# Twenty-four attention stages in two attention layers: a loop on the engines over the heads, or straight code

## The chip, the cores and the metric

The kernel runs on one core of a Trainium2 chip. A core has five engines that work side by side, each from an instruction stream of its own: TensorE (PE, matrix products; its weight loads are listed as PEld), VectorE (DVE), ScalarE (ACT), GpSimd (POOL) and SyncE (SP, which here issues the DMA transfers). They meet only through semaphores. The metric is the time of one execution on the device in microseconds (us): the median over runs, lower is better.

## The reference, cut to what matters

The input is x, of shape (2, 48, 48, 384). Two attention layers follow each other, each on a group-normalised x and with a residual:

```
x = x + attention0(group_norm(x))   # 7x7 neighbourhood mask, 16 registers as further keys
x = x + attention1(group_norm(x))   # all 2304 tokens, biases from relative positions
```

Each layer projects to queries, keys and values for 12 heads of 32 numbers, takes a softmax over the scores, weights the values with it and projects back. The first is called the local attention below, the second the full attention. With 12 heads and a batch of 2, each has 24 pairs of head and batch element: the 24 stages that this text is about.

## The kernel before, in words

The kernel is a row of phases: normalisation and projection, local attention, output mixing, then the same again with position biases and the full attention. Each phase is a block in which every engine has a stream of its own.

A stage is numbered `n = h * B + b` (head h, batch element b, B = 2). What the two attentions have in common is this. The queries of a stage are worked through in 6 units of 384. PE computes scores in two matmuls for each key tile (lines 896 and 897 local, 1570 and 1572 full). ACT takes the exponential out of PSUM (line 1047 local, 24 times a stage; line 1672 full, 54 times a stage). DVE and POOL form the low half of the probabilities (lines 1089 and 1704). PE multiplies high and low half with the values (lines 935/936 and 1596/1597). Between these, PE and DVE already find the row maxima of the next stage (lines 874/1107 and 1543/1715), so that the stages overlap, and the last steps of a stage are done within the next one.

In the local attention a row of maxima goes back to the operand `q_b` of the scores by DMA. SP issues it at line 821, in three transfers, right behind the loads of the next stage's queries, keys and values (lines 768 to 777) and the store of the last result (line 804). PE waits for it on the first scores of a stage (line 896, semaphore `rows_in`). In the full attention this row is copied by ACT (line 1660) and needs no DMA.

The order of each engine's work is the order of the code. What walks over the stages is `each_stage` (line 55), which every engine calls: SP, PE, ACT, DVE and POOL, in each of the two attentions. It writes out the stages of head 0 and of head 11 (n = 0, 1, 22, 23). The stages of heads 1 to 10 (n = 2 to 21) are a loop that runs on the engine: its body is two stages long, is written once, and is run ten times. At its end stands a conditional branch back to its start, taken nine times in each attention. Within the body the head is a register. A semaphore value or an address that depends on it has to be computed by register instructions first; these and the branch are listed under the line 59 and the lines of the waits.

Of the kernel before, what the change touches and what calls it, by code (L numbers as in the profile page):

```python
# [14 lines left out]
B, SIDE, C = 2, 48, 384  # L15
TOK = SIDE * SIDE
ALL = B * TOK
HEADS, D = 12, 32
# [35 lines left out]

def each_stage(engine, stage):

    for b in range(B):
        stage(0, b)
    with engine.Fori(1, HEADS - 1) as h:
        for b in range(B):  # L60
            stage(h, b)
    for b in range(B):
        stage(HEADS - 1, b)


def window_of(tile, size, limit):
# [583 lines left out]
def attention(nc, ctx, x, values, layer, dram, sem):  # L650
# [104 lines left out]
    with nc.Block() as block:  # L755
        @block.sync
        def _(sp):
# [80 lines left out]
            def stage(h, b):  # L838
# [12 lines left out]
                if not is_last(n):  # L851
                    place_rows(n + 1, 1 - b, False)

            each_stage(sp, stage)
            store(HEADS - 1, 1)
            for b in range(B):
# [4 lines left out]
        def _(pe):  # L861
# [149 lines left out]

            pe.wait_ge(consts_in, CONSTS)
            each_stage(pe, stage)
            for k in range(STEPS - LAG, STEPS):
                use(STAGES - 1, 1, k)
# [3 lines left out]
        def _(act):  # L1019
# [29 lines left out]
            def stage(h, b):  # L1049
                n = h * B + b  # L1050
                for k in range(STEPS):
# [3 lines left out]
                    if (k - LAG) % PER_UNIT == PER_UNIT - 1:  # L1055
                        if u >= 0:
                            take_result(h, b, u)
                        elif not is_first(n):
                            take_result(h - (1 - b), 1 - b, NA + u)

            each_stage(act, stage)
            for a in range(NA - (LAG - 1) // PER_UNIT - 1, NA):
                take_result(HEADS - 1, 1, a)
# [957 lines left out]
```

## Time and profile before

| | before |
|---|---|
| median of 3 runs | 3359.76 us (3355.78 to 3362.64) |
| the profiled execution | 3359.43 us, its span 3357.2 us |
| PE busy | 2895.1 us, 86% of the span |
| DVE busy | 2494.8 us, 74% |
| POOL / ACT busy | 57% / 55% |
| local attention, stages 2 to 21 | 331.5 to 719.85 us |
| full attention, stages 2 to 21 | 1433.0 to 3089.6 us |
| TensorE clock granted, mean over the span | 0.941 of full speed |

The page lists for each engine how long it was busy. Register, branch and semaphore instructions are not counted as busy, so an engine that is held up by its own instruction stream looks idle. In the lists of waits such time has the name "issue": the engine waited for nothing that the profile shows. A stage's start is taken here as the start of its first exponential on ACT. A window of the trace gives, for a stretch, the busy time of PE, PEld, DVE, ACT and POOL with the number of instructions, then the granted TensorE clock, the share of the DMA engines' time in use, and GB/s.

Two DMA queues called "instruction", q8 and q14, carry instructions and no data: q8 in packets of 16 KB, q14 in packets of mostly 8 KB.

### The profile page before, as it was taken

Reading aid. Unit: us, or ns where it says so; the run is one execution under the profiler, and the core shown is the slowest. Engines: PE = TensorE matmul, PEld = TensorE weight load, DVE = VectorE, ACT = ScalarE, POOL = GpSimd, SP = SyncE. Lnnn points to the kernel's source line nnn. Section 1 sums busy time; section 2 is a strip of 40 time slices with the busy share of each in tenths; the row PEclk is TensorE's granted clock in tenths of the full one; section 3 lists DMA queues with packets and bytes.
Section 4 is the critical chain, followed back from the end, with each engine's and each line's share of the span. In section 5 each row is a group of like instructions: output and inputs, shape, how many; then the busy total and the mean of one; then the engine's idle time right before and its main releaser. Section 6 shows DMA issues by size and latency. Waiting matters only on the chain. (4 is left out here: it accounts for less than half of the span.)

```text
span 3357.2 us, 94851 instructions
## 1 busy us (share of the span) xinstructions
PE 2895.1 (86%) x34200; PEld 1947.2 (58%) x34200; DVE 2494.8 (74%) x5171; ACT 1862.9 (55%) x3434; POOL 1903.2 (57%) x1561
## 2 busy tenths in 40 slices
PE   1996999997199748999999999999999999999977
PEld 1554677773155625666666666666666666666644
DVE  6745888876654537888787888888888888888854
ACT  3333666774333425666565666656565666566654
POOL 3452555550303006777777777777777777777762
PEclk9996999998599559999999999999999999999989
DMA  2425565547121984222222222222222222222114
GB/s 115 178 87 132 139 145 132 139 117 258 45 119 58 245 185 136 49 50 50 50 50 50 50 50 50 50 50 53 47 58 48 56 49 56 46 57 59 22 41 142
DMA packets 162461, 294.95 MB, mean 88 GB/s; under 512 B 78522, under 2 KB 112404, under 8 KB 156564
## 3 DMA queue, kind: packets, MB, share of 16 engines
q1 hardware_dynamic: 162052, 289.43, 33.9%
q8 instruction: 265, 4.34, 0.6%
q14 instruction: 144, 1.18, 0.1%
HBM read 189.37 MB, written 85.45 MB: 82 GB/s over the span
## 5 line engine op out<-in xcount | busy, mean ns | idle before, releaser
L1704 POOL TENSOR_TENSOR fprob_low<-fprob 128x768 f16<-128x768 f32 x1008 | 1449.7, 1466 | 563.3 <-ACT fprob L1672 562.8
L1715 DVE TENSOR_REDUCE fpart_max<-fmax_acc 128x1 f32<-128x384 f32 x2592 | 1363.8, 556 | 368.7 <-PE fmax_acc L1543 353.0
L1672 ACT ACTIVATE fprob<-fscores 128x768 f32<-128x768 f32 x1296 | 1048.2, 809 | 768.7 <-PE fscores L1572 768.6
L1543 PE MATMUL fmax_acc<-fk_m,fq_m 128*128 128x384 f16 x2592 | 853.2, 330 | 146.0 <-ACT fq_b L1660 104.8
L1570 PE MATMUL fscores<-fq_a,fk_a 128*128 128x384 f16 x2592 | 848.2, 327 | 39.5 <-issue 31.5
L1572 PE MATMUL fscores<-fq_b,fk_b 97*128 97x384 f16 x2592 | 851.4, 328 | 4.2 <-issue 4.2
L1596 PE MATMUL fout_acc<-fv,fprob 128*128 128x65 f16 x7776 | 612.0, 191 | 2.6 <-POOL fprob_low L1704 2.1
L1597 PE MATMUL fout_acc<-fv,fprob_low 128*128 128x33 f16 x7776 | 596.0, 179 | 0.9 <-issue 0.9
L1596 PEld LDWEIGHTS fout_acc<-fv,fprob 128*128 128x128 bf16 x7776 | 543.2, 97 | 68.4 <-POOL fprob_low L1704 5.1
L1597 PEld LDWEIGHTS fout_acc<-fv,fprob_low 128*128 128x128 f16 x7776 | 487.9, 96 | 52.5 <-issue 2.6
L1543 PEld LDWEIGHTS fmax_acc<-fk_m,fq_m 128*128 128x128 f16 x2592 | 251.9, 97 | 336.7 <-DVE fpart_max L1715 121.1
L1089 POOL TENSOR_TENSOR prob_low<-prob 128x242 f16<-128x242 f32 (+2 forms) x360 | 250.0, 717 | 257.1 <-ACT prob L1047 256.3
L1572 PEld LDWEIGHTS fscores<-fq_b,fk_b 97*128 97x128 f16 x2592 | 252.6, 97 | 160.9 <-issue 5.1
L1570 PEld LDWEIGHTS fscores<-fq_a,fk_a 128*128 128x128 f16 x2592 | 252.2, 97 | 135.1 <-issue 42.8
L1704 DVE TENSOR_TENSOR fprob_low<-fprob 128x768 f16<-128x768 f32 x288 | 274.7, 954 | 7.5 <-ACT fprob L1672 7.5
L1107 DVE TENSOR_REDUCE tile_max<-max_acc 128x1 f32<-128x282 f32 (+3 forms) x432 | 176.5, 435 | 75.2 <-PE max_acc L875 74.2
L410 PE MATMUL acc<-x,w_hi 128*128 128x384 f16 (+1 forms) x441 | 145.4, 332 | 83.9 <-PEq L192 83.9
L1028 ACT ACTIVATE x<-out_acc 32x384 f32<-32x384 f32 (+1 forms) x288 | 138.5, 481 | 133.4 <-PE out_acc L936 129.6
L1047 ACT ACTIVATE prob<-scores 128x266 f32<-128x266 f32 (+1 forms) x576 | 186.9, 408 | 42.8 <-PE scores L897 39.0
L896 PE MATMUL scores<-q_a,k_a 128*128 128x57 f16 (+4 forms) x1296 | 175.9, 225 | 25.1 <-DMA q_b<-max_row 21.0
L935 PE MATMUL out_acc<-prob,v 128*65 128x57 bf16 (+4 forms) x1296 | 186.3, 233 | 0.3 <-DVE x L1070 0.3
L897 PE MATMUL scores<-q_b,k_b 97*128 97x57 f16 (+4 forms) x1296 | 175.8, 225 | 0.0
(128 smaller groups left out, 3834.9 us busy)
## 6 DMA issues: line engine op xcount, KB each, us to landing
q_a<-q_hi SPq DMA_DIRECT2D x48, 432.0 KB, 5.7
fq_a<-q_hi SPq DMA_DIRECT2D x48, 432.0 KB, 7.6
q_a<-q_lo SPq DMA_DIRECT2D x24, 432.0 KB, 7.4
row_bias<-x SPq DMA_DIRECT2D x24, 432.0 KB, 7.7
col_bias<-x SPq DMA_DIRECT2D x72, 144.0 KB, 3.8
fq_a<-q_lo SPq DMA_DIRECT2D x24, 432.0 KB, 8.6
fq_a<-col_bias SPq DMA_DIRECT2D x24, 432.0 KB, 11.9
fq_b<-row_bias SPq DMA_DIRECT2D x24, 432.0 KB, 14.6
```

The source lines that it names most:

```text
L935: nc.tensor.matmul(bank[0:VW], values_of, high, start=start, stop=False)
L1047: nc.scalar.activation(dst, src, ACT.Exp).then_inc(prob_ready, 1)
L1089: last = engine.tensor_tensor(prob_low[0:p, k % RING, cut], prob[0:p, k % RING, cut], prob[0:p, k % RING, :].bitcast(BF16)[:, 1::2][:, cut ...
L1107: nc.vector.reduce_max(dst, max_acc[:, bank, 0:w], axis=AX.X).then_inc(bank_read, 1)
L1543: nc.tensor.matmul(max_acc[:, piece_bank(g, u, j), 0:PIECE], q_m[:, b, tile * 128:(tile + 1) * 128], k_m[:, b, piece * PIECE:(piece + 1) * ...
L1570: nc.tensor.matmul(bank, k_a[:, b, tile * 128:(tile + 1) * 128], q_a[:, b, tile // NA, a * UNIT:(a + 1) * UNIT], start=True, stop=False)
L1572: last = nc.tensor.matmul(bank, k_b[:, tile % NA], q_b[:, b, a * UNIT:(a + 1) * UNIT], start=False, stop=True)
L1596: nc.tensor.matmul(dst, high[:, cut], v[:, b, tile, :], start=False, stop=False)
L1597: last = nc.tensor.matmul(dst[:, D:VW], low[:, cut], v[:, b, tile, D:VW], start=False, stop=(tile == TILES - 1 and t == QT - 1))
L1672: nc.scalar.activation(prob[:, k % RING, :].rearrange("p (j n) -> p j n", j=2), scores[:, 2 * (k % 2):2 * (k % 2) + 2, 0:UNIT], ACT.Exp).t ...
L1704: engine.tensor_tensor(prob_low[:, k % RING, :], prob[:, k % RING, :], prob[:, k % RING, :].bitcast(BF16)[:, 1::2], ALU.subtract).then_inc ...
L1715: nc.vector.reduce_max(part_max[:, u % 2, j // PIECES, j % PIECES:j % PIECES + 1], max_acc[:, piece_bank(g, u, j), 0:PIECE], axis=AX.X).th ...
```

## The change

`each_stage` no longer makes a loop on the engines. It calls the code of a stage 24 times, with h and b as plain numbers, so that all 24 stages of both attentions are written out for every engine. The work of a stage and its order stay what they were.

```
 def each_stage(engine, stage):
 
-    for b in range(B):
-        stage(0, b)
-    with engine.Fori(1, HEADS - 1) as h:
+    for h in range(HEADS):
         for b in range(B):
             stage(h, b)
-    for b in range(B):
-        stage(HEADS - 1, b)
```

All line numbers behind it are four less than before: line 896 before is line 892 after.

On TensorE's stream, the end of the loop body in the full attention, before. The first two lines are the last products of an odd stage; what follows the branch, as written, is stage 22, but nine times out of ten the branch leads back to stage 2's place.

```order
8641 L1597 MATMUL fout_acc<-fv,fprob_low 128x33
8642 L1541 REGISTER_ALU
8643 L1543 MATMUL fmax_acc<-fk_m,fq_m 128x384 [waits fbank_read]
8644 L59 REGISTER_ALU
8645 L59 COMPARE_AND_BRANCH
8646 L1570 MATMUL fscores<-fq_a,fk_a 128x384 [waits fprob_ready,frow_copied,fmain_in_0]
8647 L1572 MATMUL fscores<-fq_b,fk_b 128x384
```

The same place after the change, here between an odd stage and the next even one in the middle of the 24.

```order
12757 L1593 MATMUL fout_acc<-fv,fprob_low 128x33
12758 L1539 MATMUL fmax_acc<-fk_m,fq_m 128x384 [waits fbank_read]
12759 L1566 MATMUL fscores<-fq_a,fk_a 128x384 [waits fprob_ready,frow_copied,fmain_in_0]
12760 L1568 MATMUL fscores<-fq_b,fk_b 128x384
```

The matmuls follow each other as before, with the same waits; the register instruction ahead of a wait and the branch are gone. PE's list of instructions as written grows from 10645 rows to 32470 (weight loads not listed), and 470 register instructions and both branches leave it.

TensorE's stream at the end of the loop body in the local attention, before.

```order
2154 L874 MATMUL max_acc<-k_m,q_m 128x209 [waits bank_read0]
2155 L875 MATMUL max_acc<-k_m,q_m 128x16
2156 L59 REGISTER_ALU
2157 L59 COMPARE_AND_BRANCH
2158 L896 MATMUL scores<-q_a,k_a 128x152 [waits rows_in0_0,prob_ready0,max_in0_1,main_in0_0]
```

And after.

```order
2054 L870 MATMUL max_acc<-k_m,q_m 128x209 [waits bank_read0]
2055 L871 MATMUL max_acc<-k_m,q_m 128x16
2056 L892 MATMUL scores<-q_a,k_a 128x152 [waits rows_in0_0,prob_ready0,max_in0_1,main_in0_0]
```

Here too only the control goes. The wait for the row of maxima (`rows_in0_0`) stays on the first scores of the stage.

## Rows read from the trace of the kernel before

**Rows 1.** The page: span, busy time by engine.
```profile
span 3357.2 us, 94851 instructions
...
PE 2895.1 (86%) x34200; PEld 1947.2 (58%) x34200; DVE 2494.8 (74%) x5171; ACT 1862.9 (55%) x3434; POOL 1903.2 (57%) x1561
```

**Rows 2.** Windows: us, engines busy (instructions), PEclk, DMA share, GB/s; full attention.
```profile
1352.50:1433.00 80.50, 75.85 (x998) 50.55 (x997) 68.76 (x140) 50.61 (x84) 60.47 (x43) 1.00 0.24 51
1433.00:1513.40 80.40, 75.92 (x997) 52.23 (x997) 68.64 (x139) 50.61 (x84) 60.36 (x43) 1.00 0.24 52
1513.40:3089.60 1576.20, 1453.13 (x18924) 998.68 (x18924) 1305.27 (x2623) 961.95 (x1596) 1147.73 (x799) 0.99 0.24 50
3089.60:3170.00 80.40, 75.76 (x997) 50.47 (x996) 68.68 (x140) 50.59 (x84) 60.33 (x43) 1.00 0.25 52
```

**Rows 3.** Windows, instructions of L1672 (the exponential) alone: 54 in a stage.
```profile
1513.40:3089.60 1576.20, 829.82 (x1026) 0.99 0.24 50
```

**Rows 4.** Line 59, full attention: duration ns min/median/max, first and last start us.
```profile
L59 PEldq COMPARE_BRANCH  x10: 83/3679/3924, 1592.5 to 3088.4; - x10
...
L59 DVEq COMPARE_BRANCH  x10: 55/63/74, 1593.2 to 3089.1; - x10
```

**Rows 5.** Timeline of TensorE across the first back edge: start, us, instruction, idle before.
```profile
1592.73 0.32 PE L1543 MATMUL fmax_acc<-fk_m,fq_m 128*128 128x384 f16 x1
1596.62 0.50 PE L1570 MATMUL fscores<-fq_a,fk_a 128*128 128x384 f16 x1 [3.57 <-issue]
```

**Rows 6.** Waits, 1433.1 to 3089.7: us in total, times, longest us.
```profile
PE fscores L1570 <- issue: 31.5, 9, 3.7
```

**Rows 7.** Windows at half TensorE clock behind back edges: first and last of seven.
```profile
1595.40:1602.20 6.80, 5.58 (x39) 3.17 (x40) 2.20 (x4) 1.80 (x3) 2.17 (x2) 0.50 0.02 5
...
2926.60:2930.00 3.40, 3.21 (x21) 1.84 (x22) 1.12 (x2) 0.81 (x1) 0.74 (x1) 0.50 0.03 7
```

**Rows 8.** Windows: local attention, one stage, two, eighteen, one.
```profile
311.60:331.50 19.90, 18.80 (x257) 13.49 (x255) 16.58 (x49) 13.60 (x37) 10.37 (x15) 1.00 0.59 136
331.50:371.85 40.35, 38.41 (x519) 27.54 (x517) 31.30 (x89) 27.10 (x72) 20.87 (x30) 1.00 0.57 135
371.85:719.85 348.00, 343.85 (x4651) 247.19 (x4649) 286.82 (x810) 242.79 (x648) 187.12 (x270) 1.00 0.58 139
719.85:738.95 19.10, 19.10 (x264) 13.91 (x262) 15.85 (x46) 13.43 (x37) 10.38 (x15) 1.00 0.54 127
```

**Rows 9.** Windows, instructions of L1047 (local exponential) alone: 24 in a stage.
```profile
371.85:719.85 348.00, 138.92 (x432) 1.00 0.58 139
```

**Rows 10.** Line 59, local attention.
```profile
L59 PEldq COMPARE_BRANCH  x10: 76/208/243, 370.7 to 718.9; - x10
```

**Rows 11.** Waits of TensorE: 329 to 371.5.
```profile
PE scores L896 <- DMA q_b<-max_row: 2.5, 2, 1.4
```

**Rows 12.** The same, 372 to 719.2.
```profile
PE scores L896 <- issue: 3.4, 7, 0.5
PE scores L896 <- DMA q_b<-max_row: 0.5, 1, 0.5
```

**Rows 13.** DMA queues, 371.9 to 719.9: packets, MB, share of 16 engines.
```profile
q8 instruction: 1, 0.02, 0.0%
```

**Rows 14.** The same, 331.6 to 371.9.
```profile
q8 instruction: 4, 0.07, 0.7%
q14 instruction: 5, 0.04, 0.3%
```

**Rows 15.** The same, 1433.1 to 3089.7.
```profile
q8 instruction: 189, 3.10, 0.8%
```

**Rows 16.** Line 821 (row of maxima), 343 to 352: issue to landing.
```profile
DMA to landing us min/median/max: 3.0/3.0/4.3
```

**Rows 17.** The same, 372 to 720.
```profile
DMA to landing us min/median/max: 1.6/1.9/3.2
```

**Rows 18.** Windows: the middle of a load burst of local attention.
```profile
421.00:426.00 5.00, 5.00 (x75) 3.74 (x73) 3.98 (x12) 3.16 (x10) 3.54 (x5) 1.00 1.02 220
```

## The prediction

> **What bounds the kernel now.** I read the page first: PE is busy 2895.1 of 3357.2 us, more than any other engine [rows 1], so PE's stream is what to follow. The change touches only the two attentions, so I then looked at windows of whole stages. There the trace holds its own experiment: stages 0, 1, 22 and 23 are straight code already, stages 2 to 21 are the loop, and the work of all of them is nearly the same.
>
> Full attention. The straight stages 1 and 22 take 80.5 and 80.4 us; stage 2, the loop's first, takes 80.4 [rows 2]. From the start of stage 3 to that of stage 22 it is 1576.2 us, and 1026 exponentials at 54 a stage say that this is 19 stages [rows 2, 3]: 82.96 each. The reader is to see that something in the loop costs 2.5 us a stage, and that it isn't the register arithmetic, since stage 2 has all of it and none of the cost.
>
> The branch rows show what it is. PE's branch back lasts 3679 ns in the median and 3924 at most; the shortest, 83 ns, is the one not taken [rows 4]. DVE's lasts at most 74 ns. In the timeline PE goes from the last matmul of stage 3 to the first of stage 4 with 3.57 us idle put to "issue" [rows 5], and the waits have this nine times, 31.5 us in all [rows 6]. Behind seven of the nine, PE works at half clock for 6.8 us (the first two) or 3.4 us [rows 7]: the granted clock is 0.50, which is 1.2 GHz, where it is 1.00 in straight stages. So ahead of the fall stands an idle PE, and nothing else.
>
> Local attention. PE is without a gap: 19.10 busy of 19.10 us in stage 22, 343.85 of 348.00 in stages 4 to 21 (432 exponentials, 24 a stage) [rows 8, 9]. The branch there takes 208 ns at most times and at most 243 [rows 10], and with its surroundings opens a gap of about 0.5 us: eight in that window, 3.9 us [rows 12].
>
> Why one branch takes 18 times the other shows in the queues called "instruction". In the local loop, once running, q8 moves one packet in 348 us [rows 13]: the body stays at hand. In the full loop q8 moves 189 packets of 16 KB in 1656.6 us [rows 15]. The full body is fetched anew in each of the ten passes, and the branch waits for its start. By the Trainium skill ("Runtime: NRT & Kernel Launch", "Instruction fetch mechanics") PE holds 2048 instructions, fetches ahead in sequence, and a taken branch outside what it holds stalls for the fetch; the trace agrees, with 2 x (997 + 997) records in the full body and 519 + 517 in the local one [rows 2, 8].
>
> **The change part by part.**
>
> 1. The full loop's back edges go. The first two sums check each other. By stages: 1576.2 us less 19 x 80.4 = 1527.6 leaves 48.6 us. By causes: idle PE 31.5 us [rows 6]; half clock, which gives back half of its length: windows of 6.8 us twice and of 3.4 us five times, 30.6 us, so 15.3 us. 31.5 + 15.3 = 46.8, and the rest, 0.2 us a branch, is about what the trace can't place. I take -48.6. What is late next is what bounds the straight stages: PE with 75.8 of 80.4 us busy at full clock. Nothing else fills the place, since stages 1 and 22 already show the whole of it. Bounds: -46.7 (19 stages at 80.5, as stage 1) to -50.5 (19 at 80.3, a tenth below the shortest row).
>
> 2. Register instructions go on all five engines. In the full attention they cost nothing (80.4 with them in stage 2, 80.4 without in stage 22); PE's matmuls hide them, and that cover stays. In the local attention PE has no slack. An even straight stage takes 19.10 us (stage 22), an odd one 18.8 (stage 1: 19.90, of which PE is busy 18.80; the 1.1 us is a wait that item 4 is about): 37.9 for two. The loop takes 348.0 / 9 = 38.67 for two [rows 8].
>
> 3. So the local loop control is worth 0.77 us for each two stages, the 0.5 us gap included: nine such pairs -6.9, and the first pair's back edge -0.5. Together -7.4.
>
> 4. The local attention must now fetch its instructions, all through. This is the added cost, and it lies on a path that ends late: the row of maxima comes by DMA behind the loads, and PE's first scores of each stage wait for it. In the middle of the load burst the DMA engines are full (share 1.02, 220 GB/s) [rows 18], so a packet of instructions pushes the data of one of 16 engines back. A packet's length: 189 packets at 0.8% of 16 x 1656.6 us is 1.12 us each [rows 15]. The trace has one stretch with both, the loop's first pass (stages 2 and 3), where q8 moves 4 packets and q14 5 [rows 14]. There the row lands up to 4.3 us after its issue [rows 16], against 1.6 to 3.2 later [rows 17], and PE waits for it twice, 2.5 us, the longest 1.4 [rows 11]; one of the two is the entry to the pass, the other its middle; at its end there is no such wait. In the loop this is 0.5 us once [rows 12], and that is the branch's own gap under another name.
>    From below: no such waits, 0. From above: 1.4 us at each of 18 stages, +25. The nearest row is the first pass, 1.4 at one boundary and 0 at the next, 0.7 a stage. With fewer instructions (no register arithmetic) the other engines' packets become fewer, so I take 0.5 for each of 18 stages: +9.0.
>
> By the rule of the same page and section that crossing into the next 16 KB is "mostly hidden", item 4 would be 0 and the local attention would gain the whole 7.4, a total of 3303 us; rows 16 speak against it for a transfer that shares the engines, though not for PE's own fetch, which shows no wait in straight stages.
>
> Sum: 3359.4 (the profiled execution) - 48.6 - 7.4 + 9.0 = 3312.4 us. The profiled execution lies 0.3 us under the median of the runs, 3359.76, so no correction. I forecast 3313 us, 1.4% faster.
>
> **The rivals.**
>
> A. Fetching costs nothing in the local attention. For it: stage 22 has no gap at all. Against: stage 22 loads nothing for the maxima two stages on, so its burst is shorter. 3359.4 - 48.6 - 7.4 = 3303 us.
>
> B. Fetching costs the local attention what it cost in the first pass or more: 40.35 - 0.5 = 39.85 us for two stages, 9 x (39.85 - 38.67) = +10.6, less 0.5: 3321 us; with 1.4 us at each boundary 3359.4 - 48.6 - 7.4 + 25.2 = 3329.
>
> C. The change doesn't do what it says: the stall is the cost of the next block, wherever it lies, and stands at the head of each pair of stages in straight code too. For it: the block must come from memory in either case. Against: entry into the loop, exit from it (83 ns) and the border from stage 1 to 2 show nothing of it. 3359 less the local part, about 3357 to 3361.
>
> D. Slower: PE's fetch in straight code falls behind. Up to now it does so for at most four stages at a stretch; if over 24 stages of 80 us each block came late by its own 1.12 us, then with 1994 records of PE a stage, 7.8 blocks, 20 stages would have 156 such stalls, +175 us, or some 3480 us with the gain taken off. It decides from 48.6 / 156 = 0.31 us a block. Against: within a pass of the full loop PE already runs straight through 4000 records at the same rate, with nothing under "issue" beyond the nine in the order of a us.
>
> **How the numbers follow.** The forecast (0.3 to 0.8 us a local stage) 0.5, A and what lies near it 0.25, B 0.19, C 0.02, D 0.04. What a measurement of this kernel can tell from no change is about 0.2%, 6.7 us. The forecast, A and B all lie beyond it: faster 0.94. C is "same", 0.02. D is slower, 0.04. The range goes from A less 2 us for the bound in item 1 to B's middle with 3 added: 3301 to 3325; it leaves out D, C and the far end of B.
>
> **What would show it.** In the changed profile no branch of line 59 stands on any engine. A stage of the full attention takes 80.3 to 80.6 us throughout, 20 stages about 1608 us instead of 1656.6, with the clock at 1.00 and no "issue" ahead of the scores. In the local attention two stages take 37.9 to 39.9 us; where they take more than 37.9, PE's waits name the DMA of the row of maxima, most of them 0.3 to 1.4 us long. q8 moves some 2 packets a local stage, where it moved none, and about 8 a full stage, where it moved 9. Wrong would be: stalls under "issue" every 10 us or so on PE (D), half clock within the full attention, or waits of another engine in the place of the nine stalls.

## The result and the profile after

The changed kernel takes 3311.77 us in the median of 4 runs (3308.37 to 3316.24), before 3361.20 (3355.78 to 3367.49, 4 runs). The ratio is 0.9853, 95% interval 0.9832 to 0.9874. The forecast was 3313 us. The profiled execution below took 3316.24 us, the longest of the four; the one of the kernel before took 3359.43.

The page of the changed kernel, for comparison with [rows 1]:

```profile
span 3314.4 us, 82837 instructions
...
PE 2880.5 (87%) x34200; PEld 1906.5 (58%) x34200; DVE 2490.1 (75%) x5171; ACT 1863.7 (56%) x3434; POOL 1902.0 (57%) x1561
```

The matmuls, exponentials and reductions are the same in number. The list is 12,014 instructions shorter. Counted in the two traces, 12,594 register instructions and 100 branches are gone, and 680 separate semaphore instructions have come (3134 where there were 2454).

Windows of the changed kernel, the full attention's stages 2 to 21, then the local attention's, against [rows 2, 8]:

```profile
1440.40:3048.20 1607.80, 1514.84 (x19921) 1009.26 (x19922) 1372.73 (x2761) 1012.19 (x1680) 1206.94 (x841) 1.00 0.24 51
327.20:721.90 394.70, 384.89 (x5168) 277.93 (x5165) 315.63 (x902) 271.51 (x720) 207.65 (x300) 0.99 0.58 138
```

The full attention's 20 stages went from 1656.6 us (1433.0 to 3089.6) to 1607.8, 80.39 each, at full clock: -48.8. The local attention's went from 388.35 us (331.5 to 719.85) to 394.7: +6.4. Those are the two places where the change acts.

What PE waited for in the full attention's 20 stages of the changed kernel; against [rows 6]:

```profile
PE fmax_acc L1539 <- ACT fq_b L1656: 90.4, 120, 0.8
PE fout_acc L1593 <- issue: 0.3, 1, 0.3
```

And two more of the kernel before, beside the nine of [rows 6]:

```profile
PE fscores L1572 <- issue: 4.2, 5, 0.9
PE fout_acc L1597 <- issue: 0.9, 2, 0.6
```

The nine waits of about 3.5 us are gone, these smaller ones too, and no other engine's wait came in their place. The wait for the row that ACT copies, 120 times 0.75 us, was there before (88.1 us in all) and is a part of the 80.4 us of a stage.

What PE waited for in the local attention's 20 stages, and below it the transfer that it waited for, line 817 (821 before), from issue to landing; against [rows 12, 17]:

```profile
PE scores L892 <- DMA q_b<-max_row: 9.4, 13, 1.4
```

```profile
DMA to landing us min/median/max: 1.6/2.6/4.2
```

The row of maxima now lands 2.6 us after its issue in the median, instead of 1.9 in the loop once running [rows 17], and PE stands for it 13 times. The longest of the waits in the timeline of PE:

```profile
581.73 0.23 PE L892 MATMUL scores<-q_a,k_a 128*128 128x152 f16 x1 [1.38 <-DMA q_b<-max_row]
```

Windows of two stretches right behind such waits:

```profile
503.60:507.00 3.40, 3.40 (x41) 3.03 (x40) 1.81 (x6) 2.02 (x5) 0.70 (x2) 0.51 0.26 73
582.10:588.90 6.80, 6.80 (x58) 4.57 (x56) 2.68 (x8) 3.61 (x9) 2.05 (x3) 0.50 0.18 46
```

PE is busy all through and the clock is 0.50 (1.2 GHz). Ahead of the first stood a wait of 0.94 us, ahead of the second the 1.38 us above. These two stages took 21.1 and 22.7 us, where the other eighteen took 19.5 in the mean.

The instruction queues in the local attention's 20 stages, then in the full attention's; against [rows 13, 15]:

```profile
q8 instruction: 41, 0.67, 0.7%
q14 instruction: 20, 0.16, 0.2%
```

```profile
q8 instruction: 157, 2.57, 0.7%
```

Two packets of 16 KB now fall into every local stage, where one fell into eighteen. In the full attention there are fewer than before (157 against 189); two stages now are some 4000 records on TensorE (matmuls, weight loads, register instructions), where they were some 4400.

### The profile page after: what moved, and what is told of

Its sections match the earlier page's. It is cut to its first block and busy times, and to the rows that moved or that the text cites. A ratio compares the mean times of both kernels' runs of the same rounds, so it can differ in the third digit from the quotient of the medians.

```text
span 3314.4 us, 82837 instructions
## 1 busy us (share of the span) xinstructions
PE 2880.5 (87%) x34200; PEld 1906.5 (58%) x34200; DVE 2490.1 (75%) x5171; ACT 1863.7 (56%) x3434; POOL 1902.0 (57%) x1561
## 5 line engine op out<-in xcount | busy, mean ns | idle before, releaser
L1103 DVE TENSOR_REDUCE tile_max<-max_acc 128x1 f32<-128x282 f32 (+3 forms) x432 | 176.7, 436 | 81.3 <-PE max_acc L871 80.4
```

## The experiments

Each of them sets, for each engine and each attention, whether the stages are straight code or the loop of before. The helper takes one argument more:

```
-def each_stage(engine, stage):
+def each_stage(engine, stage, straight):
+    if straight:
+        for h in range(HEADS):
+            for b in range(B):
+                stage(h, b)
+        return
     for b in range(B):
         stage(0, b)
```

Times are medians; each ratio is to runs of the kernel before on the same chip.

**TensorE alone straight in the full attention.** Edit: `each_stage(pe, stage, True)` there, `False` everywhere else.

> Full attention: TensorE's stream alone is straight code, the other four engines keep their loops; the local attention is the loop of before. Theory (the cost is TensorE's taken branch, whose target must be fetched, and the half clock behind it): the whole 48.6 us of the full attention, 3361 - 49 = about 3312 us, stages of 80.4 us. Rival (register arithmetic or loop control of the other engines has a part in it): less, for example 3330 us.

3325.18 us against 3363.62, ratio 0.9884 (0.9867 to 0.9902). Neither of the two: the gain is 38 us and not 49. The 20 full stages:

```profile
1429.60:3054.30 1624.70, 1519.76 (x19921) 1008.20 (x19922) 1371.75 (x2761) 1012.38 (x1680) 1207.89 (x841) 1.00 0.24 51
```

PE's nine stalls are gone, and the half clock but for one stretch of 3.4 us; 16.9 us over the straight 1607.8 stay. In 14.2 of them PE waits for VectorE, and the clock takes about 1.7. Two of the waits in these stages, and then the timeline of DVE behind the first back edge:

```profile
DVE fpart_max L1720 <- issue: 18.4, 9, 2.2
PE fmax_acc L1548 <- DVE fpart_max L1720: 14.2, 9, 1.7
```

```profile
1589.71 1.01 DVE L1720 TENSOR_REDUCE fpart_max<-fmax_acc 128x1 f32<-128x384 f32 x2
1592.78 2.04 DVE L1720 TENSOR_REDUCE fpart_max<-fmax_acc 128x1 f32<-128x384 f32 x4 [2.05 <-issue]
```

VectorE has a stall of 2 us of its own at each back edge, though its branch instruction is listed with 63 ns:

```profile
L64 DVEq COMPARE_BRANCH  x10: 55/63/74, 1589.8 to 3053.7; - x10
...
L64 DVEq FUSED_REGOPS  x9: 98/98/105, 1592.6 to 2894.1; - x9
```

The branch stands at 1589.8, the register instruction behind it at 1592.6. PE's branch record holds its stall, VectorE's doesn't; only the gap to the next instruction shows it. In the kernel before, it lay hidden in PE's, which was longer.

**All but TensorE straight in the full attention.**

> The other way about: in the full attention SP, ACT, DVE and POOL are straight code, TensorE keeps its loop; local attention as before. Theory: nine stalls of 3.6 us on TensorE stay, the time is that of before, 3358 to 3363 us. Rival (part of it is the other engines'): 3340 us or less.

3359.33 us against 3363.62, ratio 0.9985 (0.9975 to 0.9994). The nine waits:

```profile
PE fscores L1575 <- issue: 31.2, 9, 3.7
```

As the theory had it: nearly all of the time stays while PE's back edges stay. The 20 full stages took 1662.6 us here, 6.0 more than in the profile of the kernel before. Most of that is the clock: 44.2 us of them ran at half clock, against 30.6. With the run before it this says that the stalls lie one below the other and don't add up.

**A body of four stages, five passes.** Edit, in the full attention alone:

```
+        with engine.Fori(0, (HEADS - 2) // 2) as p:
+            for h in (p * 2 + 1, p * 2 + 2):
+                for b in range(B):
+                    stage(h, b)
```

> Full attention: the loop stays on every engine, with a body of four stages and five passes, so four taken branches instead of nine; local attention as before. Theory (a price for each taken branch, 5.4 us with the clock's part): five fewer, -27 us, about 3334 us, four waits of some 3.6 us put to issue. Rival (what costs is that the body is fetched, in proportion to its instructions, which stay the same in number): 3361 us.

3335.57 us, ratio 0.9916 (0.9899 to 0.9932). The branches of PE, and its waits:

```profile
L65 PEldq COMPARE_BRANCH  x5: 83/3657/4581, 1751.2 to 3065.8; - x5
```

```profile
PE fscores L1581 <- issue: 15.1, 4, 4.4
```

The gain is 28 us in the medians (3363.62 - 3335.57), where the theory had 27 and the rival none: the price is one for each taken branch, and not one for instructions fetched. The 20 stages took 1637.0 us, 29.2 over straight code, or 7.3 for a branch, where before it was 48.8 / 9 = 5.4. The single stalls are a little longer (3.8 against 3.5 us), and behind the four PE ran at half clock for 3.4, 3.4, 3.4 and 6.8 us, busy for 16.0 us of it. The rest are waits under "issue" away from the branches, up to 1.5 us long:

```profile
PE fout_acc L1607 <- issue: 3.3, 3, 1.5
PE fscores L1583 <- issue: 2.5, 5, 0.9
PE fout_acc L1608 <- issue: 0.4, 1, 0.4
```

15.1 + 6.2 + half of 16.0 makes 29.3, all of the 29.2. PE's instruction stream so also stood still inside a pass. In the kernel before this was 5.1 us (five and two waits, the two lines shown with the result), and in straight code 0.3. What holds it up there is not shown.

**TensorE and VectorE straight; TensorE and ScalarE straight**, both in the full attention.

> Full attention: TensorE's and VectorE's streams are straight code, ACT, POOL and SP keep their loops; local attention in its loop. With TensorE alone straight, 20 full stages took 1624.6 us instead of 1608, and VectorE stood nine times for about 2 us at its own back edge, with TensorE waiting for it (14.2 us). Theory (VectorE's back edge is what is left): 20 stages in 1608 to 1610 us, ratio to before 0.985. Rival (ScalarE's back edge, 2.5 us from the branch to the next instruction, is what is left, or takes over): 1620 us or more, ratio 0.988.

> Full attention: TensorE's and ScalarE's streams are straight code, DVE, POOL and SP keep their loops; local attention in its loop. Theory (VectorE's back edge is what is left): 20 stages in 1620 to 1625 us as with TensorE alone, ratio to before 0.988, and the nine stands of VectorE are there. Rival (ScalarE's): 1608 to 1610 us, ratio 0.985, VectorE's stands hidden or gone.

The first took 3315.37 us against 3360.97, ratio 0.9864 (0.9848 to 0.9881); the second 3326.03, ratio 0.9892 (0.9876 to 0.9909). The 20 full stages of the one and of the other:

```profile
1432.20:3049.70 1617.50, 1518.56 (x19920) 1006.69 (x19920) 1373.18 (x2761) 1012.31 (x1680) 1208.31 (x841) 1.00 0.24 51
```

```profile
1437.20:3060.50 1623.30, 1518.14 (x19920) 1007.51 (x19920) 1372.00 (x2761) 1014.12 (x1680) 1207.86 (x841) 1.00 0.24 51
```

VectorE's back edge is the next one below TensorE's, as the theory had it, but not the last: with both straight, 9.7 us stay, where the theory of the first run had 2 at most and its rival 12 or more. ScalarE stands at its back edge too. In the run with TensorE alone straight its first branch is at 1589.1 and its next instruction at 1591.6:

```profile
L64 ACTq COMPARE_BRANCH  x10: 40/45/50, 1589.1 to 3053.1; - x10
...
L64 ACTq FUSED_REGOPS  x9: 59/59/59, 1591.6 to 2893.1; - x9
```

With VectorE straight as well, this gap is 2.4 to 2.7 us, and TensorE waits nine times for GpSimd, which gets its input from ScalarE; these waits are half of the 9.7 us:

```profile
PE fout_acc L1593 <- POOL fprob_low L1709: 4.9, 9, 0.6
```

So the 48.8 us are layers: TensorE's back edges lie on top, below them VectorE's (15.5 us with TensorE and ScalarE straight: 1623.3 - 1607.8), below these ScalarE's (9.7 us with TensorE and VectorE straight). GpSimd and SyncE kept their loops in both runs. That they have no part is argued from their gaps at the branch, under 0.3 us, and not shown: no run has just the other three straight.

**The local attention alone straight.**

> The local attention alone is straight code, the full attention keeps its loop. Theory (instruction packets in the load burst make the row of maxima late, and now and then the clock falls behind such a wait): the local attention's 20 stages take 394 us against 388, so the whole is 3361 + 4 to 8 = about 3366 us. Rival (fetching is free, and only loop control goes): 3361 - 7 = 3354 us.

3367.01 us against 3363.62, ratio 1.0012 (1.0001 to 1.0024): slower by a little, on the side of the theory. The 20 local stages took 390.5 us, where it had 394, with 3.4 us at half clock. PE waited 13 times for the row:

```profile
PE scores L901 <- DMA q_b<-max_row: 8.2, 13, 1.4
```

**In the local attention TensorE alone straight, and all but TensorE**, the full attention straight.

> Full attention straight on all engines. In the local attention TensorE's stream alone is straight code, the other four keep their loops. Theory (packets of 16 KB for TensorE, 1.1 us of one DMA engine each, are what makes the row late): most of the waits for the row stay, 5 to 9 us of them, the time is that of the changed kernel, about 3310 us, and above the kernel whose local attention is all loop (about 3305). Rival (the smaller packets of the other engines do it): waits of 0 to 2 us, 3301 us.

> Full attention straight on all engines. In the local attention all but TensorE are straight code. Theory: few waits for the row (0 to 2 us), nine branches of 0.2 us on TensorE, the time of the kernel whose local attention is all loop, about 3305 us. Rival (the smaller packets do it): waits of 5 us and more, 3312 us.

3309.22 us, ratio 0.9849 (0.9835 to 0.9862), and 3306.62, ratio 0.9834 (0.9820 to 0.9847). The intervals overlap, so the times alone decide nothing; the traces do. The 20 local stages and PE's waits with TensorE alone straight:

```profile
325.20:717.40 392.20, 383.29 (x5168) 276.58 (x5166) 318.93 (x901) 270.22 (x720) 208.03 (x300) 1.00 0.58 139
```

```profile
PE scores L901 <- DMA q_b<-max_row: 8.6, 10, 1.6
```

and with all but TensorE straight:

```profile
329.40:716.30 386.90, 380.96 (x5168) 274.88 (x5165) 314.61 (x899) 270.56 (x720) 207.61 (x300) 1.00 0.58 139
```

```profile
PE scores L901 <- issue: 4.1, 9, 0.5
PE scores L901 <- DMA q_b<-max_row: 3.1, 3, 1.4
```

TensorE's 16 KB packets are what makes the row late; the other engines' smaller ones hardly do. Of the three waits that stay in the second, two (1.29 and 1.38 us) are at the entry to the loop's first pass and in its middle, where TensorE's body is fetched once; the third, 0.48 us, is the branch's own gap under another name. The kernel before has the same two, of 1.10 and 1.39 us.

**Four kernels side by side**: the changed kernel again; the full attention straight and the local in its loop; and each of these two with the local attention's store of the last result moved behind the row of maxima in SP's order:

```
-                if not is_first(n):
-                    store(h - (1 - b), 1 - b)
                 if not is_last(n):
                     place_rows(n + 1, 1 - b, False)
+                if not is_first(n):
+                    store(h - (1 - b), 1 - b)
```

> The changed kernel itself, as the yardstick for the three beside it: 3312 us.

> The full attention is straight code, the local attention keeps its loop of before. Theory: the gain of the one without the loss of the other; the changed kernel's 20 local stages took 394.7 us against 388.3, so 6 us less than the changed kernel, about 3305 us. Rival (the local attention's longer time is chance, or lies in the phases between): the same as the changed kernel, 3312, or up to 3316 if loop control counts.

> All straight code as in the changed kernel, and in the local attention SP issues the store of the last result (297 KB) behind the row of maxima instead of ahead of it. Theory (the row lands late because it is queued behind a burst that instruction packets have lengthened): 297 KB at some 220 GB/s are 1.35 us, the row lands that much earlier, the twelve waits (9.2 us) and the falls of the clock behind them (5 us) go: 3312 - 14 = about 3298 us. Rival (TensorE waits at the stage's start for its own instructions, not for the row): no change, 3312 us.

> Local attention in the loop of before, full attention straight, and the store behind the row as in the run beside it. Theory: in the running loop the row came in time anyway, so this gains nothing over the same kernel with the store ahead, about 3305 us, and is 6 to 7 us above the all-straight kernel with the store moved, whose stages lack the loop control (0.77 us for two stages). Rival: the store ahead of the row costs something in the loop too: 3300 us or less.

| kernel | median, us | ratio to before (95%) | 20 local stages, us |
|---|---|---|---|
| changed kernel | 3309.56 | 0.9856 (0.9839 to 0.9873) | 391.2 |
| local in its loop | 3307.06 | 0.9855 (0.9838 to 0.9871) | 387.8 |
| all straight, store behind | 3300.18 | 0.9832 (0.9817 to 0.9848) | 383.1 |
| local in its loop, store behind | 3305.77 | 0.9845 (0.9829 to 0.9860) | 386.8 |

PE's waits in the changed kernel and in the third:

```profile
PE scores L892 <- DMA q_b<-max_row: 7.4, 11, 1.0
```

```profile
PE scores L901 <- DMA q_b<-max_row: 3.1, 6, 1.0
```

The third is the fastest version found: 9.4 us under the changed kernel in the medians. The run ranges do not touch (3295.84 to 3303.81 against 3305.70 to 3310.51), though the two intervals to before overlap in part. With 297 KB taken out from ahead of the row, 4.3 us of the waits go and so does the half clock (6.8 us of it in this run of the changed kernel, none in the third), and 20 local stages take 8.1 us less. The rival, that PE waits for its own instructions at a stage's start, is out: moving a transfer of data would not have moved that. The expected 14 us were too many, since some waits stay and this run of the changed kernel had less half clock to lose. In the loop the same move gave 1.3 us in the medians, inside the runs' scatter, as expected. The all-straight kernel with the store behind lies 5.6 us below the one with the local loop and the same move, where 6 to 7 were expected, though the runs of the two overlap.

The 6 us between the changed kernel and the one with the local loop came out as 2.5 us in the medians, with intervals that are nearly the same. The windows show 3.4 us (391.2 against 387.8); the rest of the first comparison was what one profiled execution adds to another. The other profiled executions point the same way. With the store in its place, the local loop took 387.5 to 392.1 us in seven kernels (389.0 in the mean), straight code 390.5, 391.2 and 394.7 (392.1): straight is 3.1 us longer in the mean, and single executions overlap. Two of the loops, too, had 10.2 us at half clock, at the first pass.

## Why the prediction was right

**The full attention (item 1), -48.6.** Measured -48.8. The sum stood on stages that were straight code already within the same trace, and these said rightly what all would become: 80.39 us a stage against 80.4.

The second sum, by causes, came near (46.8) with two errors that partly cancel. It left out the 5.1 us under "issue" within the passes, and it counted idle PE twice: of the 30.6 us at half clock PE was busy for 26.8, so 13.4 us go to the clock and not 15.3. Put right, it gives 50.0. The same two terms fit all four profiled executions in which TensorE looped here, in us over the straight 1607.8:

| full attention | "issue" | half of PE's busy time at half clock | sum | measured |
|---|---|---|---|---|
| kernel before | 36.6 | 13.4 | 50.0 | 48.8 |
| all but TensorE straight | 38.2 | 18.8 | 57.0 | 54.8 |
| all loop, local straight | 39.2 | 22.3 | 61.5 | 58.9 |
| four stages a body | 21.3 | 8.0 | 29.3 | 29.2 |

So the loop's cost is no fixed number. Behind the same nine branches the clock was at half for 30.6, 44.2 and 54.4 us in three executions, and the profile that the forecast was read from had the least. Straight code took 1607.5 to 1608.1 us in all seven executions.

The attribution beside it was too simple. The text put everything to TensorE's branch and read VectorE's 74 ns as the whole of its price. A change on TensorE alone brought 32 of these us in the windows (1656.6 - 1624.7), or 38 in the medians, where straight code on all engines of the full attention alone brought 49 (3356.39 - 3307.06). The number came out right because the change makes all engines straight.

**Register arithmetic (item 2).** Nothing in the full attention, as said: stage 2 has it and takes 80.4 us, and the kernel that has lost it on four engines, all but TensorE, gained nothing in the 20 full stages (1662.6 us against 1656.6, with 5.4 of the 6.0 us put to the clock in the table).

**Local loop control (item 3), -7.4, and fetching (item 4), +9.0.** The forecast for the 18 stages was 0.5 us of waiting in each, 9.0 us; measured were 9.4 us over 20 stages in this execution, and 7.4 and 8.2 in two others. The mechanism is shown by the runs: packets of TensorE's instructions in the load burst, a late row, a wait at the stage's start. What the sum did not have is the clock that falls behind the longer of these waits: 3.4 and 6.8 us at half speed, 5.1 us in the profiled execution, 3.4 in the other. So the 20 local stages rose by 6.4 us where the two items make +1.6, and the other execution gave +2.9.

Item 3 was well sized: with the store behind the row, the loop took 386.8 us without a wait for the row, and straight code 383.1 us with 3.1 us of such waits, so that loop control is worth 6.8 us in all.

Rival A (fetching is free, 3303 us) is refuted by the queues and the waits; the rule "mostly hidden" of the Trainium skill ("Runtime: NRT & Kernel Launch", "Instruction fetch mechanics") holds for TensorE's own issue in straight code, 0.3 us under "issue" in 20 full stages, and not for a transfer in the same DMA engines. Rival B had the mechanism right and its price too high: +10.1 us at its near end, where the profiled execution has +6.4.

**Rivals C and D.** No stall moved into the straight code (C), and PE did not fall behind its fetch over 24 stages (D). Against D the prediction said that nothing stood under "issue" beyond the nine in the order of a us; the trace of before has four such waits, of 0.89 us each.

**The span, and what was luck.** 3357.2 - 3314.4 = 42.8 us, of which the 40 stages explain 42.4. Between the two attentions the changed kernel's profiled execution takes 5 us more, in phases that the change doesn't touch (523.7 us against 518.6); that stretch scatters by up to 5 us among the executions of the kernels above, with no order in it. It is offset by the stages 0 and 1 of the local attention, the start and the tail. So the profiled pair differs by 43 us and the medians by 49. The forecast lacked the clock in the local attention (5.1 us) and the profiled execution came out 3.8 us above its 3312.4; the median of the four runs lies 4.5 us below that execution. That 3313 is within 1.2 us of the median is therefore luck in part.

## What to carry to other kernels

Look for the stages that a loop has peeled off: in the same trace they show what straight code would cost. A loop whose body stays at hand costs little (here 6.8 us in 20 stages) and keeps the DMA engines free of instructions; one that is too long pays at every taken branch, on each engine by itself, and the engines' stalls hide each other, so that curing one shows the next. Where straight code streams through full DMA engines, put nothing that can wait ahead of a small transfer that the bottleneck waits for.

## What the runs showed of the hardware

- A taken branch of TensorE back over some 4400 records (matmuls, weight loads and register instructions) stalled 3.3 to 3.9 us, and back over twice as many up to 4.6; over some 1150 it took 0.2 us, and one packet was fetched in 348 us.
- VectorE stood about 2 us at the same back edge with a body of 555 records, ScalarE 2.4 to 2.9 us with 403. GpSimd with 170 went on within 0.3 us (with 338, in the body of four stages, it stood for 3.1 to 3.9), and so did VectorE and ScalarE in the local loop, with 166 and 148. Their branch records say 40 to 74 ns all the same.
- A wait of 0.94 us was followed by 3.4 us at half clock and one of 1.38 us by 6.8 us, in a stretch where PE was busy otherwise; a wait of 1.14 us at 663 us was not followed by any, nor one of 1.39 us in the kernel before. What decides it the runs don't show.
